# Loads between the halves of the stores, another order up to the second unit, and a last unit that ends in column parities over six banks

## The chip, the core and the metric

The kernel runs on one core of a Trainium2 chip. The core has five engines that each work through an instruction list of their own and meet at semaphores: PE (TensorE, matmul), DVE (VectorE), ACT (ScalarE), POOL (GpSimd) and SP (SyncE, which here only issues DMAs). The metric is the device time of one launch in microseconds (us). A profiled execution comes with a trace, from which all rows below are read.

## The reference

Two layers. Layer 0 takes x of shape (4, 256, 64, 64), convolves it 7x7 with dilation 2 to 128 channels, maps these to 49 logits for each pixel, takes a softmax over the 49, and sums the 49 shifted copies of x with these weights:

```python
k = conv(x, w1, padding=6, rhs_dilation=2) + b1
k = conv(k, w2) + b2                       # 1x1, 49 outputs
attn = softmax(k, axis=1)
y0 = einsum('bkchw,bkhw->bchw', shifts(x, 49), attn)
```

Layer 1 adds to y0 a gelu of `yc + y0 * D`, where `yc` comes from a linear recurrence over the 64 columns, and takes a layernorm over the 256 channels with a scale and a shift:

```python
y = gelu(yc.T[None, :, None, :] + x * D[None, :, None, None])
o = layernorm_over_channels(x + y) * ln_w + ln_b
```

## The kernel before

Both weights of layer 0 are folded into one 7x7 convolution with 48 outputs (softmax needs only differences of logits). Since the dilation is 2, even and odd rows are independent: the work falls into eight **units** (4 images x 2 row parities), unit n being image n // 2, parity n % 2. x of a unit lies in `raw0` or `raw1` by parity. The convolution runs over transformed rows (a scheme that trades multiplications for sums of rows): DVE and POOL build eleven arrays from `raw` (`make_u1` and its like, lines 1028 to 1041 and 313), ACT writes the f16 high part of each (`v_high`, line 700) and DVE the low part (`v_low`, line 1110), in a ring of four buffers `V`. PE convolves them in `conv(n, first, last)`, 49 steps in seven blocks of seven (line 438). Block b waits for the arrays that it reads and, in the first unit, for the weights' low parts (`weights_low`, line 1436; `weights_high` is ACT's, line 866).

What follows the convolution of unit m = n - 1 is done beside the convolution of unit n:

1. logits from the sums (`logits_*`, lines 1149 and 1158), turned by PE (`turn_logits`, line 457), gathered by DVE (1208, 1210), exponentials on ACT, sixteen small ones (737), division and a high and a low half (742, 1230), turned again (467) and copied to `AT` (746);
2. `spread(m, r)`, ten rows r: PE spreads the weights to a banded matrix in one of two PSUM banks `wk` (478), ACT casts it (`band_high`, 751), DVE makes the rest (`band_low`, 1235);
3. `apply(m, y)`, eight of them (495): PE multiplies the band with the turned x (`XT`) into one of two banks; y runs over row half q, channel half h, column parity w. ACT evicts each (`attended`, 760), DVE makes the arguments of gelu (1250), ACT the gelu (766), DVE the residual (1256);
4. the layernorm: POOL sums the channel halves (338, 344), PE the channels with a matrix of ones (`mean` 509, `variance` 516), DVE centres and normalises (1263, 1269), ACT squares, inverts and applies scale and shift (773, 781, 787). The second half of unit m ends in unit n + 1.

SP issues all loads of x and all stores, in one written order. In `unit(n)` it waits until unit n - 1's x is no longer read (`pool_rows`, `xt_done`), loads x of unit n + 1, and then waits four times for the output of unit n - 1 (`affine`) and stores it, two DMAs for each row half. So the load of x(n + 2) stands behind the second half of these stores. Readers of a new x are, in this order on their engines: ACT's `bound` (line 725, the largest absolute value, between `band_high` 4 and 5, and 6 and 7), from which POOL's all-reduce (309) and DVE's `scales` (1116) follow, and DVE's `make_u1` (1028, between `band_low` 2 and 3).

The **first unit** has the weights' preparation in front and in between: composites on PE (603), row sums on DVE (1367, `row_sums`), x turned by PE (`turn_x`, 529) with ACT's and DVE's halves behind (731, 1139). PE turns x in eight places from step 16 of the convolution on. The order of all engines there is written out by hand, as it is in `unit`.

The **last unit** has no convolution beside its steps 1 to 4. Its layernorm works in quarters (`last_centre`, `last_squares`, `last_rstd`, `last_normalise`, `last_affine`).

## Time and profile before

| | |
|---|---|
| median of 3 runs | 895.67 us (894.84 to 896.17) |
| profiled execution | 896.21 us, its span 894.4 us |
| PE busy | 803.0 us (90%) |
| DVE busy | 722.4 us (81%) |
| ACT busy | 519.9 us (58%) |
| POOL busy | 188.4 us (21%) |
| share of PE in the chain that ended last | 51% |
| DMA of x in that chain | 7% |
| mean granted clock of TensorE | 0.947 of full speed |

The span is what the trace covers from the first to the last instruction; 1.8 us of the profiled execution lie around it. A share of busy time is an average over three stretches that differ: the first unit (until about 146 us), six units with a period of some 97 us, of which five are followed by another load, and the end of the last one (from about 820 us), where PE has no convolution. What a change is worth is read in each of them. In a timeline a number in brackets is the time that the engine waited before the row, and behind the arrow stands what ended it ("issue": nothing that the trace shows).

### The profile page before, as it was taken

The page shows a single profiled execution, that of the slowest core. Times are in us where ns is not written, and L with a number is a line of the kernel's source. Part 1 is how long each engine was busy: PE and PEld are TensorE (multiplying, and loading weights), DVE is VectorE, ACT ScalarE, POOL GpSimd, SP SyncE. Part 2 cuts the span into 40 slices and gives each one's busy share as a digit, 9 for nine tenths or more (in the row PEclk, how much of TensorE's full clock was granted, in tenths as well). Part 3 has the DMA queues.
Part 4 walks back from the last instruction along what each step waited for, and adds up shares of the span by engine and source line. Part 5 has one row for each costly group of instructions (what it writes and reads, how often), then busy time and mean ns, then how long its engine had stood idle before and what let it go on. Part 6 is the DMA issues. An engine that isn't in the chain of part 4 may idle for free.

```text
span 894.4 us, 27128 instructions
## 1 busy us (share of the span) xinstructions
PE 803.0 (90%) x12261; PEld 493.8 (55%) x12261; DVE 722.4 (81%) x876; ACT 519.9 (58%) x834; POOL 188.4 (21%) x100
## 2 busy tenths in 40 slices
PE   4979787999997999899997999899989999996485
PEld 4975333575555655565564645565546655663451
DVE  3899769889995999689986999599967999677336
ACT  2363232766674666665584767557665659465546
POOL 3114102112510233013311151024301341021010
PEclk9999889999997999999997999999997999999588
DMA  9322005000125010700151011601070011002103
GB/s 312 72 52 45 2 2 95 2 3 2 48 53 92 3 48 2 143 3 1 49 113 33 2 48 42 104 1 40 11 143 2 1 49 50 3 1 64 32 1 94
DMA packets 133597, 41.78 MB, mean 47 GB/s; under 512 B 133145, under 2 KB 133226, under 8 KB 133226
## 3 DMA queue, kind: packets, MB, share of 16 engines
q1 hardware_dynamic: 132248, 40.01, 19.9%
q8 instruction: 96, 1.57, 0.7%
q10 hardware_dynamic: 1234, 0.04, 0.1%
q14 instruction: 19, 0.16, 0.1%
HBM read 23.27 MB, written 16.78 MB: 45 GB/s over the span
## 4 chain that ended last, share of the span: by engine, by line
PE 51%; DVE 15%; issue 12%; ACT 11%; DMA 8%; POOL 1%; SPq 1%; DVEq 0%; ACTq 0%; POOLq 0%
PE cv L438 26%; DMA raw<-in_x_dram 7%; PE wk L495 6%; PE pcomp L603 5%; PE wk L478 4%; PE ms L516 3%; ACT chs L737 3%; ACT V L700 3%; PE wk L529 2%; DVE R L1028 2%; DVE tg L1250 2%; PE wk L457 2%; DVE V L1110 1%; DVE XT L1139 1%; DVE Z L1158 1%
## 5 line engine op out<-in xcount | busy, mean ns | idle before, releaser
L438 PE MATMUL cv<-V,W 128*32 128x496 f16 (+6 forms) x7840 | 447.1, 383 | 19.7 <-issue 7.5
L438 PEld LDWEIGHTS cv<-V,W 128*32 128x32 f16 (+1 forms) x7840 | 201.5, 97 | 224.7 <-issue 41.6
L313 POOL TENSOR_TENSOR R<-raw 128x1152 f32<-128x1152 f32 x32 | 100.2, 3130 | 258.4 <-DVE V L1110 93.8
L700 ACT ACTIVATE V<-R,sc 128x1024 f16<-128x1024 f32 (+1 forms) x88 | 110.5, 1274 | 55.1 <-PE cv L438 54.3
L1110 DVE SCALAR_TENSOR_TENSOR V<-R,sc,V 128x1024 f16<-128x1024 f32 (+1 forms) x88 | 122.4, 1399 | 9.7 <-ACT V L700 9.6
L478 PE MATMUL wk<-AT,sel 128*128 128x16 f16 x2560 | 85.1, 192 | 23.1 <-DVE band L1235 21.2
L495 PE MATMUL wk<-band,XT 128*128 128x224 f16 (+1 forms) x960 | 102.9, 268 | 2.6 <-DVE band L1235 1.4
L478 PEld LDWEIGHTS wk<-AT,sel 128*128 128x128 f16 x2560 | 79.6, 103 | 44.7 <-DVE band L1235 29.6
L495 PEld LDWEIGHTS wk<-band,XT 128*128 128x128 f16 x960 | 83.3, 99 | 25.5 <-issue 5.3
L1235 DVE TENSOR_TENSOR band<-wk,band 128x512 f16<-128x512 f32 x80 | 54.7, 689 | 44.0 <-ACT band L751 43.8
L751 ACT CAST band<-wk 128x512 f16<-128x512 f32 x80 | 46.7, 584 | 69.4 <-PE wk L478 68.4
L731 ACT ACTIVATE XT<-wk,sc 128x512 f16<-128x512 f32 x64 | 42.9, 681 | 53.6 <-PE wk L529 52.9
L760 ACT ACTIVATE o<-wk,sc 128x512 f32<-128x512 f32 x64 | 45.7, 730 | 46.7 <-PE wk L495 46.6
L1041 DVE SCALAR_TENSOR_TENSOR R<-R 128x1024 f32<-128x1024 f32 (+1 forms) x56 | 72.5, 1298 | 0.2
L1028 DVE SCALAR_TENSOR_TENSOR R<-raw 128x512 f32<-128x512 f32 (+1 forms) x48 | 48.2, 1047 | 27.5 <-DMA raw<-in_x_dram 27.4
L1139 DVE SCALAR_TENSOR_TENSOR XT<-wk,sc,XT 128x512 f16<-128x512 f32 x64 | 47.2, 746 | 16.5 <-ACT XT L731 16.3
L338 POOL TENSOR_TENSOR chs<-o 128x1024 f32<-128x1024 f32 x14 | 36.7, 2622 | 110.4 <-DVE o L1256 95.1
L344 POOL TENSOR_TENSOR chs<-tg 128x1024 f32<-128x1024 f32 x14 | 34.5, 2462 | 96.3 <-ACT tg L773 96.3
L603 PE MATMUL pcomp<-w2t,w1raw 128*128 128x48 f32 x196 | 45.0, 418 | 9.4 <-DMA w1raw<-in_L_conv_w_dram 9.4
L1250 DVE SCALAR_TENSOR_TENSOR tg<-o,dcol,yc 128x1024 f32<-128x1024 f32 x32 | 40.4, 1279 | 13.4 <-ACT o L760 13.1
L529 PEld LDWEIGHTS wk<-id,raw 128*128 128x128 f32 x256 | 35.1, 208 | 27.9 <-issue 14.2
L603 PEld LDWEIGHTS pcomp<-w2t,w1raw 128*128 128x128 f32 x196 | 43.7, 312 | 10.0 <-issue 9.6
(138 smaller groups left out, 903.1 us busy)
## 6 DMA issues: line engine op xcount, KB each, us to landing
raw<-in_x_dram SPq DMA_DIRECT2D x16, 1024.0 KB, 11.5
out_dram<-o SPq DMA_DIRECT2D x28, 512.0 KB, 3.9
w1raw<-in_L_conv_w_dram SPq DMA_DIRECT2D x2, 3136.0 KB, 16.8
out_dram<-o SPq DMA_DIRECT2D x8, 256.0 KB, 3.4
cm<-in_L_conv_Cmat_dram ACTq DMA_DIRECT2D x1, 32.0 KB, 8.4
dcol<-in_L_conv_D_dram ACTq DMA_DIRECT2D x2, 0.5 KB, 9.8
lnw<-in_L_conv_ln_w_dram ACTq DMA_DIRECT2D x2, 0.5 KB, 7.2
lnb<-in_L_conv_ln_b_dram ACTq DMA_DIRECT2D x2, 0.5 KB, 7.2
```

Source lines behind the costliest of these rows:

```text
L313: nc.gpsimd.tensor_tensor(R[buffer][:, :, :, :], rows_of(par, j + 2), rows_of(par, j), ALU.subtract).then_inc(pool_rows, 1)
L438: ins = pe.matmul(to.rearrange("p (w t c) -> p w t c", w=2, c=COLS)[:, :, :, c0:c1], W[:, ws, h * K7 + v, k0:k1], slot(n, a)[:, low, :, t0 ...
L478: ins = pe.matmul(wk[:, r % 2, c * TILES:(c + 1) * TILES].rearrange("p (w j) -> p w j", w=2), sel[:, s, f:f + P], AT[:, :, r:r + 29:4, c], ...
L495: ins = pe.matmul(wk[:, y % 2, (r0 - 16 * q) * COLS:(r1 - 16 * q) * COLS], XT[:, xl, 8 * w + j, h, :], band[:, bl, 8 * w + j, r0 - 4 * j + ...
L603: last = pe.matmul(pcomp[:, g % 3, v * P:v * P + REL], w1h[:, u * K7 + v, :], w2t[:, 0:REL], start=True, stop=True)
L700: nc.scalar.activation(v_array(n, a, 0), array(a), ACT.Identity, scale=sc[:, par, 3:4]).then_inc(vhi, 1)
L1028: nc.vector.scalar_tensor_tensor(out=R[buffer][:, 0:wins, h, :], in0=raw[par][:, h, r:r + 4 * wins - 3:4, :], scalar=-4.0, in1=raw[par][:, ...
L1041: nc.vector.scalar_tensor_tensor(out=part(*out), in0=part(*a), scalar=factor, in1=part(*b), op0=ALU.mult, op1=ALU.add).then_inc(row_made, 1)
L1110: nc.vector.scalar_tensor_tensor(out=v_flat(n, a, 1), in0=array_flat(a), scalar=sc[:, par, 3:4], in1=v_flat(n, a, 0), op0=ALU.mult, op1=AL ...
L1139: nc.vector.scalar_tensor_tensor(out=low, in0=wk[:, g % 2, :], scalar=sc[:, par, 3:4], in1=high, op0=ALU.mult, op1=ALU.subtract).then_inc( ...
L1235: nc.vector.tensor_tensor(band[:, 1, :, r, :], wk[:, r % 2, :].rearrange("p (c t) -> p t c", t=TILES), band[:, 0, :, r, :], ALU.subtract). ...
L1250: nc.vector.scalar_tensor_tensor(out=tg[:, h], in0=o[:, q, h], scalar=dcol[:, h:h + 1], in1=yc[:, h].unsqueeze(1).broadcast_to([P, 16, WID ...
```

## The change

Three parts, in one diff.

**A. SP.** `store` now stores one row half. Behind the first half of unit n - 1's output SP waits for `xt_done` and `pool_rows` and loads x of unit n + 2; the second half of the stores comes behind it.

**B. The first unit.** PE turns x before the convolution and earlier inside it, DVE and ACT do their parts of the same work in another order: `relative_bias` later, the turned x's low halves earlier, the rows of unit 1 before the last weights, `scales(1, 1)` before `v_low(0, 0, 10)`. ACT's bound of x(1) still waits for all weights. No arithmetic is added.

**C. The end of the last unit.** The two halves of the softmax go through separately, the second half's logits turned into `cv`, which the convolution no longer needs; PE runs 22 and 9 idle matmuls between (`keep_running`, their result is overwritten); `spread` and `apply` use six banks in place of two; ACT's eviction `attended` is gone, and DVE makes the arguments of gelu and the residual straight from PSUM for each of the eight column parities (`last_args`, `last_residual`, 128x512 each in place of four of 128x1024); gelu goes in eight parts.

The diff, cut to its core:

```diff
-            def unit(n, par, b_load, b_out):
+            def next_load(n, par, b):
                 sp.wait_ge(pool_rows, POOL_ROWS * n)
                 sp.wait_ge(xt_done, 8 * n)
-                load(n + 1, 1 - par, b_load)
-                store(n, par, b_out)
+                load(n + 1, 1 - par, b)
...
             load(1, 1, 0)
-            for n in range(1, UNITS - 1):
-                unit(n, n % 2, (n + 1) // 2, (n - 1) // 2)
-            store(7, 1, 3)
+            next_load(1, 1, 1)
+            for n in range(1, UNITS):
+                store(n, n % 2, (n - 1) // 2, 0)
+                if n < UNITS - 2:
+                    next_load(n + 1, (n + 1) % 2, (n + 2) // 2)
+                store(n, n % 2, (n - 1) // 2, 1)
...
-                if r >= 2:
-                    pe.wait_ge(blo, 10 * m + r - 1)
+                banks = 6 if m == LAST else 2
+                if r >= banks:
+                    pe.wait_ge(blo, 10 * m + r - banks + 1)
...
-            conv(0, 0, 16, cold=True)
-            for g in range(8):
-                turn_x(0, 0, g, cold=True)
-                conv(0, 16 + 4 * g, 20 + 4 * g, cold=True)
+            turn_x(0, 0, 0, cold=True)
+            turn_x(0, 0, 1, cold=True)
+            conv(0, 0, 6, cold=True)
+            turn_x(0, 0, 2, cold=True)
...
+            def keep_running(w):
+                if w == 0:
+                    pe.wait_ge(l_soft, 2)
+                for _ in range(IDLE_MATMULS[w]):
+                    pe.matmul(wk[:, 0, 0:5 * 2 * REL], id16[:, :], W[:, 0, 0:5, :].rearrange("p s k -> p (s k)"),
+                              start=True, stop=True)
...
+            def last_high(w):
+                act.wait_ge(l_soft, (13, 17)[w])
+                nc.scalar.copy(HL[:, w * WIN:(w + 1) * WIN, 0:TAPS], E[:, w * WIN:(w + 1) * WIN, :]).then_inc(l_hi, 1)
...
+            def last_args(y):
+                h, w = y // 2 % 2, y % 2
...
+                dve.wait_ge(y_done, 8 * m + y + 1)
+                nc.vector.scalar_tensor_tensor(out=tg[:, h, :, w:WIDTH:2],
+                                               in0=apply_bank(m, y).rearrange("p (r c) -> p r c", c=COLS),
+                                               scalar=ds[:, h:h + 1],
+                                               in1=yc[:, h, w:WIDTH:2].unsqueeze(1).broadcast_to([P, 16, COLS]),
+                                               op0=ALU.mult, op1=ALU.add).then_inc(l_args, 1)
```

What stands on the engines at three places. First SP, from the load of x(2) on; `raw` is x, `out_dram<-o` a store. Before:

```order
L274 DMA raw<-in_x_dram 128x32x64 [waits x_turned,pool_rows]
L274 DMA raw<-in_x_dram 128x32x64
L280 DMA out_dram<-o 128x16x64 [waits affine_done] x4
L274 DMA raw<-in_x_dram 128x32x64 [waits x_turned,pool_rows]
L274 DMA raw<-in_x_dram 128x32x64
L280 DMA out_dram<-o 128x16x64 [waits affine_done] x4
```

And now, on SP at the same place:

```order
L287 DMA raw<-in_x_dram 128x32x64 [waits x_turned,pool_rows]
L287 DMA raw<-in_x_dram 128x32x64
L293 DMA out_dram<-o 128x16x64 [waits affine_done] x2
L287 DMA raw<-in_x_dram 128x32x64 [waits x_turned,pool_rows]
L287 DMA raw<-in_x_dram 128x32x64
L293 DMA out_dram<-o 128x16x64 [waits affine_done] x4
```

The load of x(3) has moved from behind four stores to behind two; the same holds for x(4) to x(7).

Second, DVE late in the first unit, where the scales of x(1) are made (1116 before, 1209 now, which waits for POOL's all-reduce `amax_all`). Before (1139 is the turned x's low half, 1028 rows of x(1)):

```order
L1110 SCALAR_TENSOR_TENSOR V<-R,sc,V 128x2x512 [waits rows_made,v_high]
L1028 SCALAR_TENSOR_TENSOR R<-raw 128x9x64 [waits v_low,raw_in_odd,borders_set]
L1028 SCALAR_TENSOR_TENSOR R<-raw 128x9x64
L1028 SCALAR_TENSOR_TENSOR R<-raw 128x8x64 [waits rows_made]
L1028 SCALAR_TENSOR_TENSOR R<-raw 128x8x64
L1036 TENSOR_TENSOR R<-R 128x1024 [waits rows_made,v_low]
L1036 TENSOR_TENSOR R<-R 128x1024 [waits rows_made]
L1158 SCALAR_TENSOR_TENSOR Z<-ev,Z 128x16x32 [waits logit_steps]
L1158 SCALAR_TENSOR_TENSOR Z<-Z 128x16x32 [waits logit_steps]
L1158 SCALAR_TENSOR_TENSOR Z<-ev,Z 128x16x32 [waits logit_steps]
L1158 SCALAR_TENSOR_TENSOR Z<-Z 128x16x32 [waits logit_steps]
L1116 TENSOR_SCALAR sc<-aall 128x1 [waits amax_all]
```

And now, on DVE from the last low half of the weights (1531) on:

```order
L1531 SCALAR_TENSOR_TENSOR W<-wc,wsc,W 128x7x16
L1203 SCALAR_TENSOR_TENSOR V<-R,sc,V 128x1152 [waits rows_made,v_high]
L1244 SCALAR_TENSOR_TENSOR ev<-cv,sc,ev 32x512 [waits logit_steps,block_convolved,sums_copied]
L1244 SCALAR_TENSOR_TENSOR Z<-cv,sc,ev 128x16x32 [waits logit_steps,block_convolved]
L1244 SCALAR_TENSOR_TENSOR ev<-cv,sc,ev 128x512 [waits logit_steps,block_convolved]
L1253 SCALAR_TENSOR_TENSOR Z<-ev,Z 128x16x32 [waits logit_steps]
L1253 SCALAR_TENSOR_TENSOR Z<-Z 128x16x32 [waits logit_steps]
L1124 TENSOR_TENSOR R<-R 128x1024 [waits rows_made,v_low]
L1209 TENSOR_SCALAR sc<-aall 128x1 [waits amax_all]
```

The rows of x(1) have moved ahead of the last weights, and the instruction that waits for `amax_all` stands eight rows behind these weights, where before the rows of x(1) and four combinations of logits (1158) came in between; `v_low(0, 0, 10)`, which stood ahead of it, now follows it.

Third, PE at the end of the last unit, from the turned logits to the first `spread`. Before:

```order
L457 MATMUL wk<-id,Z 128x128 [waits x_turned_low,logit_steps]
L457 MATMUL wk<-id,Z 128x128 x7
L457 MATMUL wk<-id,Z 128x128 [waits softmax_steps]
L457 MATMUL wk<-id,Z 128x128 x7
L467 MATMUL ms<-id,HL 128x128 [waits normed,softmax_steps]
L467 MATMUL ms<-id,HL 128x128 x7
L467 MATMUL ms<-id,HL 128x128 [waits normed,softmax_steps]
L467 MATMUL ms<-id,HL 128x128 x7
```

And now, on PE (699 are the idle matmuls, 705 the turned weights of one half each):

```order
L690 MATMUL wk<-id,Z 128x128 [waits x_turned_low,logit_steps]
L690 MATMUL wk<-id,Z 128x128 x7
L690 MATMUL cv<-id,Z 128x128 x8
L699 MATMUL wk<-W,id 128x480 [waits last_softmax_steps]
L699 MATMUL wk<-W,id 128x480 x21
L705 MATMUL cv<-id,HL 128x128 [waits last_softmax_steps]
L705 MATMUL cv<-id,HL 128x128 x7
L699 MATMUL wk<-W,id 128x480 x9
L705 MATMUL cv<-id,HL 128x128 [waits last_softmax_steps]
L705 MATMUL cv<-id,HL 128x128 x7
```

The second half's logits no longer wait for the first half's gather, and thirty-one idle matmuls have come in.

## Rows read from the trace of the kernel before

**Rows 1.** Windows: us; busy (xcount) of PE, PEld, DVE, ACT, POOL; PEclk, DMA share, GB/s
```profile
835.60:852.30 16.70, 12.38 (x336) 11.59 (x336) 6.91 (x10) 7.79 (x12) 0.00 (x0) 0.50 0.01 3
```

**Rows 2.** Waits of DVE, 245 to 735 us: us in total, times, longest us
```profile
DVE R L1028 <- DMA raw<-in_x_dram: 27.4, 5, 5.9
```

**Rows 3.** Waits of PE, 245 to 735 us
```profile
PE wk L478 <- DVE band L1235: 19.4, 5, 5.1
PE cv L438 <- issue: 2.3, 2, 1.5
```

**Rows 4.** Timeline of SP: start us, us, engine line op out<-in xcount [idle before <-releaser]
```profile
231.37 33.21 SPq L280 DMA_DIRECT2D out_dram<-o  x4
264.68 6.08 SPq L274 DMA_DIRECT2D raw<-in_x_dram  x2
```

**Rows 5.** Timeline of PE, unit 1
```profile
157.14 14.78 PE L438 MATMUL cv<-V,W 128*32 128x480 f16 x280
...
234.91 0.74 PE L529 MATMUL wk<-id,raw 128*128 128x128 f32 x4
```

**Rows 6.** Timeline of PE, unit 2
```profile
249.08 14.78 PE L438 MATMUL cv<-V,W 128*32 128x480 f16 x280
```

**Rows 7.** Timeline of PE, unit 7
```profile
735.70 14.78 PE L438 MATMUL cv<-V,W 128*32 128x480 f16 x280
...
773.85 6.24 PE L495 MATMUL wk<-band,XT 128*128 128x224 f16 x60
```

**Rows 8.** Timeline of DVE, unit 2
```profile
256.30 2.35 DVE L1269 TENSOR_TENSOR o<-o,ms 128x1024 f32<-128x1024 f32 x2
...
279.25 1.43 DVE L1028 SCALAR_TENSOR_TENSOR R<-raw 128x576 f32<-128x576 f32 x2 [5.49 <-DMA raw<-in_x_dram]
```

**Rows 9.** Waits of DVE, 47 to 149 us
```profile
DVE XT L1139 <- ACT XT L731: 9.2, 4, 4.2
DVE V L1110 <- ACT V L700: 6.3, 4, 3.2
```

**Rows 10.** Timeline of POOL, unit 1
```profile
189.38 0.37 POOL L309 PARTITION_ALL_REDUCE aall<-amx  x1 [22.44 <-ACT tg L725]
197.00 2.87 POOL L313 TENSOR_TENSOR R<-raw 128x1152 f32<-128x1152 f32 x1 [7.24 <-issue]
```

**Rows 11.** Timeline of ACT, first unit
```profile
117.65 1.90 ACT L725 ACTIVATE tg<-raw 128x2048 f32<-128x2048 f32 x1
...
119.54 1.30 ACT L700 ACTIVATE V<-R,sc 128x1152 f16<-128x1152 f32 x1
```

**Rows 12.** Timeline of DVE, first unit
```profile
120.88 1.42 DVE L1110 SCALAR_TENSOR_TENSOR V<-R,sc,V 128x1152 f16<-128x1152 f32 x1 [2.34 <-ACT V L700]
...
123.39 0.75 DVE L1149 SCALAR_TENSOR_TENSOR Z<-cv,sc,ev 128x512 f32<-128x512 f32 x1
...
132.15 2.49 DVE L1036 TENSOR_TENSOR R<-R 128x1024 f32<-128x1024 f32 x2
134.55 0.69 DVE L1158 SCALAR_TENSOR_TENSOR Z<-ev,Z 128x512 f32<-128x512 f32 x1
```

**Rows 13.** Timeline of PE, start of unit 1 behind the first unit
```profile
148.01 4.88 PE L438 MATMUL cv<-V,W 128*32 128x512 f16 x60 [2.99 <-DVE Z L1149]
```

**Rows 14.** Timeline of PE, last unit
```profile
838.68 2.10 PE L478 MATMUL wk<-AT,sel 128*128 128x16 f16 x64 [1.17 <-ACT AT L746]
841.22 2.10 PE L478 MATMUL wk<-AT,sel 128*128 128x16 f16 x64 [0.44 <-DVE band L1235]
...
852.36 8.89 PE L495 MATMUL wk<-band,XT 128*128 128x224 f16 x60 [1.40 <-DVE band L1235]
```

**Rows 15.** Timeline of ACT, last unit
```profile
826.95 0.34 ACT L737 ACTIVATE chs<-chs,st 128x49 f32<-128x49 f32 x1 [1.20 <-DVE st L1218]
...
875.59 1.28 ACT L1010 ACT_TABLE_LOAD   x1
876.89 0.66 ACT L987 ACTIVATE cv<-cv,eps 128x512 f32<-128x512 f32 x1
```

More of the change, by code:

```diff
@@ L190, in conv_seq_kernel @@
         ms16 = ms[:].bitcast(F16)
+        cv16 = cv[:].bitcast(F16)
+        last_banks = [wk[:, 0, :], wk[:, 1, :]] + [cv[:, i, :] for i in range(4)]
+        spread_bank = lambda m, r: last_banks[r % 6] if m == LAST else wk[:, r % 2, :]
+        apply_bank = lambda m, y: last_banks[(0, 1, 4, 5, 2, 3, 0, 1)[y]] if m == LAST else wk[:, y % 2, :]
+        var_bank = lambda i: cv[:, (i + 2) % 4, :]
         s_w1 = [sem("w1_in_0"), sem("w1_in_1")]
@@ L486, in apply @@
                     pe.wait_ge(blo, 10 * m + 10)
-                if y >= 2:
+                if m == LAST and y >= 6:
+                    pe.wait_ge(l_res, y - 5)
+                if m < LAST and y >= 2:
                     pe.wait_ge(xs_made, 8 * m + y - 1)
@@ L706, in sum_copy @@
                     act.wait_ge(z_step, steps)
+                if not n:
+                    act.wait_ge(s_bias, 4)
+                    act.wait_ge(scale_steps, SCALES)
                 add = bias[:, :] if s == M1P else 0.0
@@ L779, in inverse_deviation @@
                 act.wait_ge(var_done, 2 * m + q + 1)
+                if m == 0 and q == 0:
+                    act.wait_ge(s_const, 2)
                 both = ms[:].rearrange("p a b -> p (a b)")
@@ L861, in weights_high @@
             def weights_high(first, last):
+                if first == 0:
+                    act.wait_ge(amax_part, 2)
+                    act.wait_ge(s_wscale, 12)
                 for s, h in HIGH_ORDER[first:last]:
@@ L968, in _, with last_exponentials, last_turned, last_gelu @@
             m = UNITS - 1
-            inverse_deviation(m - 1, 1)
+            def last_exponentials(w, first, last):
+                act.wait_ge(l_soft, 5 * w + 5)
+                for i in range(w * WIN + first, w * WIN + last):
+                    nc.scalar.activation(E[:, i, :], E[:, i, :], ACT.Exp, bias=st[:, 1, i:i + 1],
+                                         accum_out=st[:, 2, i:i + 1]).then_inc(l_exp, 1)
+            def last_high(w):
+                act.wait_ge(l_soft, (13, 17)[w])
+                nc.scalar.copy(HL[:, w * WIN:(w + 1) * WIN, 0:TAPS], E[:, w * WIN:(w + 1) * WIN, :]).then_inc(l_hi, 1)
+            def last_turned(w):
+                act.wait_ge(ht_ready, 2 * m + w + 1)
+                nc.scalar.copy(AT[:, w, PAD:PAD + ROWS, :].rearrange("p r c -> p (r c)"), cv16[:, 2 + w, :]).then_inc(
+                    at_copy, 1)
+            def last_gelu(y):
+                h, w = y // 2 % 2, y % 2
+                act.wait_ge(l_args, y + 1)
+                nc.scalar.activation(tg[:, h, :, w:WIDTH:2], tg[:, h, :, w:WIDTH:2], ACT.Gelu).then_inc(l_gelu, 1)
+            inverse_deviation(m - 1, 1)
+            last_exponentials(0, 0, 8)
+            last_exponentials(1, 0, 4)
+            last_high(0)
+            last_exponentials(1, 4, 8)
+            last_turned(0)
+            last_high(1)
+            last_turned(1)
+            band_high(m, 0)
+            band_high(m, 1)
             scale_shift(m - 1, 1, 0)
+            band_high(m, 2)
+            band_high(m, 3)
             scale_shift(m - 1, 1, 1)
-            exponentials(m, 0, 16)
-            attention_high(m)
-            turned_attention(m, 0)
-            turned_attention(m, 1)
-            for r in range(BROWS):
+            for r in range(4, BROWS):
                 band_high(m, r)
@@ L1050, in make_u1 @@
                 for h in range(HALVES):
+                    if not n:
+                        dve.wait_ge(first_in[h], 16)
                     u_half(0, par, h, 2, 0, 9)
@@ L1129, in logit_scales @@
             def logit_scales(n, par):
+                if not n:
+                    dve.wait_ge(s_mask, 2)
                 nc.vector.tensor_scalar(sc[:, par, 4:5], sc[:, par, 1:2], winv[:, :], 1 / X_SCALE, ALU.mult,
@@ L1469, in _ @@
             weight_scales()
-            for h in range(HALVES):
-                dve.wait_ge(first_in[h], 16)
-            dve.wait_ge(s_border, 2)
             make_u1(0, 0)
@@ L1502, in _ @@
+            turned_x_low(0, 0, 0)
+            relative_bias()
+            turned_x_low(0, 0, 1)
+            weights_low(4, 11)
+            turned_x_low(0, 0, 2)
             v_low(0, 0, 4)
+            weights_low(11, 12)
+            turned_x_low(0, 0, 3)
+            weights_low(12, 14)
+            make_y2_plus(0)
             v_low(0, 0, 5)
-            make_y2_plus(0)
+            turned_x_low(0, 0, 4)
+            v_low(0, 0, 6)
+            weights_low(14, 15)
             make_y2_minus(0)
-            weights_low(12, 16)
@@ L1526, in _ @@
             logits_2(0, 0)
+            logits_rows(0, True)
+            make_x1_plus(1)
+            scales(1, 1)
             v_low(0, 0, 10)
-            dve.wait_ge(s_border, 4)
-            make_u1(1, 1)
-            make_u0(1, 1)
-            make_x1_plus(1)
+            logit_scales(1, 1)
             make_x1_minus(1)
-            logits_rows(0, True)
+            make_u2(1, 1)
             logits_rows(0, False)
-            scales(1, 1)
-            logit_scales(1, 1)
-            turned_x_low(0, 0, 5)
@@ L1568, in last_centre @@
                 dve.wait_ge(q_mean, i + 1)
-                dve.wait_ge(o_made, 4 * m + (2 if i < 2 else 4))
+                dve.wait_ge(l_res, 4 if i < 2 else 8)
                 for h in range(HALVES):
```

285 lines of the change are left out of this document (182 added, 103 removed).

## The prediction

> **What bounds the kernel now.** I read the shares on the page first (PE busiest, DVE next), then the windows by stage, since the three parts of the change lie in stages with different limits, then the waits in each stage, and at last the timelines at the places that the change moves.
>
> In the units PE is the bound but for one gap. From 245 to 735 us the waits of DVE have one entry that is large: five waits, one in each of units 2 to 6, for a load of x, 27.4 us in all [rows 2]. The waits of PE have its echo: 19.4 us in five waits for DVE's `band_low` [rows 3]. The reader is to see why in SP's timeline: the load follows the fourth store in the same row of the queue, at 264.68, though the first stores stood there at 231.37 [rows 4]. PE had turned the last of the old x at 234.91 + 0.74 = 235.65 [rows 5], and from then on the buffer was free. DVE stood at `make_u1` from 273.76 and went on at 279.25 [rows 8].
>
> In the first unit nobody is the bound alone. DVE waits 9.2 us for ACT's turned x and 6.3 us for ACT's `v_high` [rows 9], which wait for PE in turn; unit 1 starts on PE at 148.01, behind DVE [rows 13]. At the end PE, ACT and DVE hand each other small pieces; the windows show PE's clock at half there, 0.50 of full (1.2 GHz), from 835.6 to 852.3, though PE is busy 12.38 of 16.70 us [rows 1].
>
> **A, the load of x, units 2 to 6.** Two units show what a unit takes when x is there in time. The same place in the program, the 280 matmuls from step 5 on, begins at 157.14 in unit 1, at 249.08 in unit 2 and at 735.70 in unit 7 [rows 5 to 7]. Unit 1, whose x(2) had been loaded early, took 249.08 - 157.14 = 91.94 us. Units 2 to 6 took (735.70 - 249.08) / 5 = 97.32 each. The difference, 5.38 us, is more than PE's wait of 19.4 / 5 = 3.9, because the clock falls after the wait. Five units: 26.9 us.
>
> Is unit 1 a fair pattern? It lacks the second half of the layernorm of the unit before; on DVE that is two instructions, 2.35 us [rows 8], on ACT and PE about as much. They stand well ahead of `make_u1`, where the next wait is one for exponentials, so I take nothing off for them; if they came onto the path, 2.35 x 5 = 11.8 would be gone. Unit 1 also has no load in flight. In units 2 to 6 PE has two pauses with no releaser, 2.3 us together [rows 3]. In future PE has no slack to hide such pauses, and I keep them whole: 26.9 - 2.3 = 24.6. On SP the two issues of the load, 6.08 us [rows 4], stand ahead of the second stores, which were not through before 264.68; with its issues from 235.65 to 241.7 the load is out of their way. The load itself comes 264.68 - 235.65 = 29.0 us earlier, against the 5.49 that were missing, so there are some 23 us to spare. Bounds of A: 12.8 (the layernorm's share and the pauses both lost) and 27.4, DVE's whole wait.
>
> On the pauses the Trainium skill, page "SBUF — State Buffer", section "SBUF: two separate sides", holds that DMA ports and engine ports cannot slow each other. By that rule A would be the full 26.9; the two pauses are of the sequencer and not of data, so the rule may be right and the pauses stay all the same.
>
> **B, the first unit.** The work is conserved; DVE has no pause but 9.2 + 6.3 = 15.5 us of waits [rows 9]. Since unit 1 begins when DVE is through, B is worth the waits that vanish, less those that come. All turned-x waits are of PE's late `turn_x`; in the new order PE turns early and DVE's pieces are due when their inputs are old. But one new wait stands out. ACT's bound of x(1) still needs the last low half of the weights, and DVE's `scales(1, 1)` now stands soon behind it. From the last low half: bound 1.9 + 0.2, `v_high` 1.30, bound again [rows 11] (the second as the first), together 5.3; then the all-reduce. Its own row is 0.37 long, but POOL's next instruction, which waits for nothing new, comes 7.6 us after its start [rows 10]. That makes 12.9. On DVE meanwhile: `v_low` 1.42, three sums at 0.75, two combinations at 0.69 and one `make_x1_plus` at 1.24 [rows 12], 6.3 in all. DVE would stand 6.6 us, and behind it queue `v_low(0, 0, 10)`, on which PE's last block waits, and everything for unit 1. One more us for small new waits, which I can't place: 15.5 - 6.6 - 1.0 = 7.9. Bounds: if the all-reduce's result is out after its own 0.37 us, it comes 5.3 + 0.4 = 5.7 behind the weights, before DVE is there at 6.3, and B is 14.5; if PE and ACT's new places (ACT now waits for a turned x ahead of weights) cost as much as they bring, B is 0, and a little below it, -3, if one such wait of 3 us is left. I take the middle one, since POOL's gap is the nearest row.
>
> **C, the last unit.** Three steps, on the way to the table load at 875.59, behind which the quarters go on as before: the inversion starts at 876.89 [rows 15], and from it to the end of the execution I change nothing.
> 1. From the turned logits to the first `spread`. Before, the first exponential is at 826.95 [rows 15] and the first spread at 838.68 [rows 14], 11.7 apart: sixteen exponentials at 0.33 are 5.2, the rest 6.5. Now the first half's exponentials need only the first gather (they start some 4.0 earlier, as the second half's turning, its gather and two layernorm instructions of 2.35 in all [rows 8] are no longer ahead), and behind the sixteenth only the second half's pieces remain, each half as long, about 4.1. That is 4.0 + 2.4 = 6.4.
> 2. Ten spreads. Two take 2.10 and then wait 0.44 for a bank [rows 14], so ten with what follows took 852.36 - 838.68 = 13.7. With six banks 10 x 1.05 + 1.3 for the last cast and low half = 11.8. Gain 1.9. ACT has two late scale-and-shifts among its casts; a cast is shorter than a spread, and it catches up.
> 3. From the first `apply` to the table load: before 875.59 - 852.36 = 23.2. Now eight applies at 6.24 / 4 = 1.56, the rate of unit 7 [rows 7], are 12.5, one mean of ones 1.1 among them, then an argument 0.75, a residual 0.75, a centring 1.3 and the squares 1.3 (512 columns at 0.65 to 0.75, as rows 12 and 15): 17.7. Gain 5.5. DVE has 16 pieces of 0.75 = 12.0, just under PE's 12.5.
>
> That is 13.8. It holds only at full clock. Four applies took 8.89 right behind the spreads, against 6.24 [rows 7, 14]: 2.65 for the half clock. The spreads did not raise the clock before [rows 1], there are ten of them in a row again, and the idle matmuls end before them. I take it that the clock is down again when `apply` begins: C = 13.8 - 2.65 = 11.2. Bounds: 14 above; below 5, if DVE, which now has evictions too, paces step 3 and nothing is gained in it. The idle matmuls cost nothing if they are over when the halves come; an apply has 15 matmuls of 237 columns in the mean (96 to 320) in 1.56 us, so one of 480 takes 0.21 and 22 take 4.6, in a gap of some 6 (first gather to first half's weights).
>
> **Sum.** The profiled execution is 896.21. 896.21 - 24.6 - 7.9 - 11.2 = 852.5. The median of the runs shown lies 0.5 below that execution, so 852.
>
> **Rivals.**
> - *Everything mild goes well*, 0.2: the clock stays at full through the spreads (+2.65), the all-reduce is soon out (+6.6), the pauses vanish (+2.3): 840.5. For it: before, PE had next to nothing to do between the turned logits and the turned weights, and the idle matmuls now fill that. Against: rows 1 show a busy PE that stays at half. The Trainium skill, page "TensorE: Matmul & The Clock Gate", section "What's actually happening", says that throttled is the default and that activity releases it; by it PE would keep the full clock from the idle matmuls on, and C alone would be 13.8.
> - *The layernorm's second half takes the place of the load*, 0.12: A is 24.6 - 11.8 = 12.8, 864. Against: unit 7 has that half too and its first `apply` comes 773.85 - 735.70 = 38.15 after the mark [rows 7], without wait for it.
> - *The first unit's order brings nothing*, 0.1: 860. For it: ACT now has in-order waits for turned x in front of weights that DVE needs.
> - *The last unit is paced by DVE*, 0.1: C is 5, 858.
> - *The load does not come earlier after all*, 0.02: SP reaches it only when `xt_done` is there, which might be late; A is 0, 877. Rows 5 and 8 speak against.
> - *Slower*, 0.03: the load now runs beside the end of one unit and the start of the next. If a load in flight kept PE from its instructions, PE would stand for its length. From issue to DVE's going on a load took 279.25 - 264.68 = 14.6 [rows 4, 8]; five are 73, against 43.7 gained: 925. It decides from 43.7 / 5 = 8.7 us a load on. Against: the pauses come to 0.5 a load now.
>
> **How the numbers follow.** My forecast, 852, has 0.43, with 846 to 858 as its own range. A difference under 0.2%, 1.8 us, can't be told from no change here; no case but a mixture reaches it. Faster 0.96, same 0.01, slower 0.03. The range holds forecast, the good case and the three bad ones in part: 838 to 865.
>
> **What would show it.** SP's load at the end of PE's eighth turned x and no wait of DVE's `make_u1` for a DMA; marks 92 to 93 us apart in units 2 to 6 (97.3 would refute A, 94.5 be the layernorm). Unit 1 starting about 140 on PE, and on DVE a wait of some 6 us ahead of `scales(1, 1)`. In the last unit the first spread some 6 us sooner behind the turned logits, the table load some 17 behind the first apply, and the clock in the window of the first applies: 0.5, or else 1.0. A PE busy share that does not rise to about 93% or more would mean that the time went elsewhere.

## The result, and the profile after

The changed kernel takes 834.11 us (833.27 to 835.22, four runs) against 895.92 for the kernel before on the same chip: 0.9305 of it, with a 95% interval of 0.9277 to 0.9332. The forecast was 852, and 834.11 lies below its range. The profiled execution took 833.81 us, 62.4 less than that of before, with a span of 832.0. In its profile PE is busy for 95% of the span and DVE for 87%.

The timeline of PE gives the marks again (start us, us, engine line op out<-in xcount [idle before <-releaser]). The mark of a unit is the start of its 280 matmuls from step 5 on, the same place in each unit's program. Shown are those of units 1, 2 and 7, and behind them the last unit's first spread, the first apply matmuls and their followers.

```profile
135.62 14.78 PE L454 MATMUL cv<-V,W 128*32 128x480 f16 x280
226.73 14.78 PE L454 MATMUL cv<-V,W 128*32 128x480 f16 x280
...
686.50 14.78 PE L454 MATMUL cv<-V,W 128*32 128x480 f16 x280
...
783.64 2.11 PE L495 MATMUL wk<-AT,sel 128*128 128x16 f16 x64 [1.10 <-ACT AT L1051]
...
794.86 4.81 PE L514 MATMUL wk<-band,XT 128*128 128x224 f16 x30 [1.41 <-DVE band L1330]
799.51 6.23 PE L514 MATMUL cv<-band,XT 128*128 128x224 f16 x60
```

Beside [rows 5 to 7] they divide the 62.4 us over the parts:

- up to the mark of unit 1: 157.14 - 135.62 = 21.5 (B, forecast 7.9)
- unit 1 itself: 91.94 before, 91.11 now: 0.8 (forecast 0). With one part alone it takes 91.97 to 91.99 (e1, e2 and e3 below), so no part gives this by itself, and its cause stays open
- units 2 to 6: (686.50 - 226.73) / 5 = 91.95 each against 97.32, so 26.8 (A, forecast 24.6)
- from the mark of unit 7 to the end of the span: 894.4 - 735.70 = 158.7 before, 832.0 - 686.50 = 145.5 now: 13.2 (C, forecast 11.2)

So the miss of 18.7 us (62.4 for a forecast of 43.7) is 13.6 from B, 2.2 from A, 2.0 from C and 0.8 from unit 1.

**A.** The timeline of SP answers to [rows 4].

```profile
209.02 3.47 SPq L293 DMA_DIRECT2D out_dram<-o  x2
213.38 5.37 SPq L287 DMA_DIRECT2D raw<-in_x_dram  x2
238.80 3.43 SPq L293 DMA_DIRECT2D out_dram<-o  x2
```

The load stands between the halves of a store, and it is issued as PE's eighth turned x ends (at 212.55 + 0.75 = 213.30), as the prediction asked. The waits of DVE in units 2 to 6 (226 to 687 us) hold no DMA any more ([rows 2] had 27.4 us), and the waits of PE have neither `band` nor a pause without a releaser ([rows 3] had 19.4 and 2.3). The largest entry of DVE now, and both entries of PE:

```profile
DVE band L1330 <- ACT band L814: 21.7, 29, 1.7
```
```profile
PE wk L548 <- DVE XT L1234: 4.3, 5, 0.9
PE ms L528 <- POOL chs L354: 1.2, 5, 0.2
```

The reader is to see that a large wait (21.7 us of DVE, for ACT's casts) stands beside a PE that waits for next to nothing.

**B.** The windows show DVE's way from the scales of unit 0 into unit 1, before and after (us; busy of PE, PEld, DVE, ACT, POOL; PEclk, DMA share, GB/s).

```profile
47.80:147.80 100.00, 79.89 (x1081) 46.12 (x1080) 83.19 (x135) 38.84 (x51) 17.55 (x10) 0.95 0.21 38
```
```profile
47.70:126.40 78.70, 74.48 (x1089) 46.06 (x1092) 75.06 (x134) 40.54 (x56) 17.15 (x10) 1.00 0.32 55
```

Both windows end some 0.65 us ahead of the same `v_low` (148.43 before, 127.07 now). The second is 21.3 us shorter, and in two ways: DVE's idle time went from 16.8 to 3.6 us (13.2), and its busy time, for the same work but one instruction of 0.75, from 83.19 to 75.06 (8.1). Of the 3.6 us of idle time that are left 2.4 are waits for ACT's `v_high`, 0.3 is the one for the all-reduce, and the rest lies between rows; the waits for turned x are gone.

**C.** These are the steps of the prediction. The first spread came 838.68 - 735.70 = 102.98 behind the mark of unit 7 and comes 97.14 behind it (5.8, forecast 6.4). Ten spreads with what follows took 13.7 and take 11.2 (2.5, forecast 1.9). From the first apply to the table load it was 23.2 and is 813.26 - 794.86 = 18.4 (4.8, forecast 5.5 less 2.65 for the clock). In the timeline of ACT:

```profile
813.26 1.28 ACT L1098 ACT_TABLE_LOAD   x1
814.55 0.66 ACT L1084 ACTIVATE cv<-cv,eps 128x512 f32<-128x512 f32 x1
```

From there to the end 17.5 us pass, as before. The windows of the last unit show the granted clock: full while the idle matmuls run, half again through the spreads and into the first applies.

```profile
772.00:783.60 11.60, 8.16 (x52) 4.00 (x50) 8.96 (x21) 8.97 (x37) 0.00 (x0) 1.00 0.01 2
783.60:794.90 11.30, 9.85 (x321) 9.75 (x322) 6.64 (x10) 8.53 (x13) 0.00 (x0) 0.54 0.39 96
794.90:799.50 4.60, 4.60 (x30) 3.41 (x31) 0.75 (x1) 1.05 (x2) 0.00 (x0) 0.64 0.00 0
799.50:805.60 6.10, 6.10 (x65) 5.19 (x63) 5.50 (x8) 2.64 (x5) 0.00 (x0) 1.00 0.02 4
```

### The profile page after: what moved, and what is told of

It reads as the page before. It is cut to its first block, busy times and chain, and to the rows that moved or that the text cites. A ratio compares the mean times of both kernels' runs of the same rounds, so it can differ in the third digit from the quotient of the medians.

```text
span 832.0 us, 27209 instructions
## 1 busy us (share of the span) xinstructions
PE 790.7 (95%) x12292; PEld 492.6 (59%) x12292; DVE 721.3 (87%) x892; ACT 514.8 (62%) x831; POOL 189.4 (23%) x100
## 4 chain that ended last, share of the span: by engine, by line
PE 59%; DVE 24%; issue 7%; ACT 7%; DMA 1%; POOL 1%; DVEq 0%; SPq 0%; ACTq 0%
PE cv L454 32%; PE wk L495 7%; PE pcomp L622 5%; DVE tg L1345 3%; PE ms L535 3%; DVE Z L1253 3%; PE wk L514 3%; PE wk L548 3%; DVE R L1116 3%; DVE V L1203 2%; DVE XT L1234 2%; DVE R L1124 2%; DVE Z L1244 2%; PE wk L473 1%; ACT tg L788 1%
## 5 line engine op out<-in xcount | busy, mean ns | idle before, releaser
L454 PE MATMUL cv<-V,W 128*32 128x496 f16 (+6 forms) x7840 | 429.9, 374 | 3.1 <-DVE V L1203 2.2
L514 PE MATMUL wk<-band,XT 128*128 128x224 f16 (+1 forms) x900 | 95.9, 267 | 1.4 <-DVE band L1330 1.4
L514 PEld LDWEIGHTS wk<-band,XT 128*128 128x128 f16 x900 | 77.6, 99 | 23.0 <-issue 5.1
L495 PEld LDWEIGHTS wk<-AT,sel 128*128 128x128 f16 x2368 | 73.6, 100 | 18.7 <-issue 16.6
L1330 DVE TENSOR_TENSOR band<-wk,band 128x512 f16<-128x512 f32 x74 | 51.0, 690 | 35.3 <-ACT band L814 34.9
L495 PE MATMUL wk<-AT,sel 128*128 128x16 f16 x2368 | 78.7, 192 | 1.1 <-ACT AT L1051 1.1
L814 ACT CAST band<-wk 128x512 f16<-128x512 f32 x74 | 43.1, 582 | 46.0 <-PE wk L495 45.0
L823 ACT ACTIVATE o<-wk,sc 128x512 f32<-128x512 f32 x56 | 40.1, 731 | 33.7 <-PE wk L514 33.6
L1116 DVE SCALAR_TENSOR_TENSOR R<-raw 128x512 f32<-128x512 f32 (+1 forms) x48 | 52.7, 1140 | 0.0
L548 PE MATMUL wk<-id,raw 128*128 128x128 f32 x256 | 43.3, 303 | 6.8 <-DVE XT L1234 5.1
L622 PEld LDWEIGHTS pcomp<-w2t,w1raw 128*128 128x128 f32 x196 | 43.7, 312 | 9.8 <-issue 9.4
```

The source lines that it names most:

```text
L454: ins = pe.matmul(to.rearrange("p (w t c) -> p w t c", w=2, c=COLS)[:, :, :, c0:c1], W[:, ws, h * K7 + v, k0:k1], slot(n, a)[:, low, :, t0 ...
L495: ins = pe.matmul(spread_bank(m, r)[:, c * TILES:(c + 1) * TILES].rearrange("p (w j) -> p w j", w=2), sel[:, s, f:f + P], AT[:, :, r:r + 2 ...
L514: ins = pe.matmul(apply_bank(m, y)[:, (r0 - 16 * q) * COLS:(r1 - 16 * q) * COLS], XT[:, xl, 8 * w + j, h, :], band[:, bl, 8 * w + j, r0 - ...
L548: ins = pe.transpose(wk[:, g % 2, c:c + P], rows[:, w:4 * WIDTH:2], id32[:, :])
L622: last = pe.matmul(pcomp[:, g % 3, v * P:v * P + REL], w1h[:, u * K7 + v, :], w2t[:, 0:REL], start=True, stop=True)
L1116: nc.vector.scalar_tensor_tensor(out=R[buffer][:, 0:wins, h, :], in0=raw[par][:, h, r:r + 4 * wins - 3:4, :], scalar=-4.0, in1=raw[par][:, ...
```

## The experiments

The theory: the 13.6 us that B brought beyond its forecast have two sources. The result of the all-reduce is out as soon as its row ends, and DVE's rows are no longer held while GpSimd (POOL) works. The rivals: the 13.6 come from another part of the change, or the rows are shorter for another reason.

### One part at a time

e1, the kernel before with SP's part (A) alone:

```
-            def store(n, par, b):
-                for q in range(2):
...
+            next_load(1, 1, 1)
+            for n in range(1, UNITS):
+                store(n, n % 2, (n - 1) // 2, 0)
+                if n < UNITS - 2:
+                    next_load(n + 1, (n + 1) % 2, (n + 2) // 2)
+                store(n, n % 2, (n - 1) // 2, 1)
```

> The kernel before with part A alone (SP's queue: each load of x between the two halves of a store). After's marks give part A 26.9 us (unit pitch 97.32 before, 91.95 after). If the parts add up, this one is at 895.7 - 26.9 = 869, with a pitch of 91.9 to 92.0 in units 2 to 6, a first unit and a last unit as before. If part A needs the other two (the layernorm's second half comes onto the path without them), the pitch is 94 or more and the time 880 or more.

868.19 us (866.28 to 868.71), 0.9701 of before (0.9671 to 0.9730), before at 895.22. That is 27.0 us, with the mark of unit 2 at 248.82 and of unit 7 at 707.72: a pitch of 91.8. A needs nothing of the rest, and the layernorm's second half doesn't come onto the path.

e2, the kernel before with the new order of ACT, DVE and PE up to the second unit alone:

```
-            conv(0, 0, 16, cold=True)
-            for g in range(8):
-                turn_x(0, 0, g, cold=True)
...
+            turn_x(0, 0, 0, cold=True)
+            turn_x(0, 0, 1, cold=True)
+            conv(0, 0, 6, cold=True)
...
```

> The kernel before with part B alone (the order of ACT, DVE and PE up to the second unit). My theory now: part B is worth 21 to 22 us (13 of waits, 8 of DVE instructions that no longer run beside one of POOL's), so 874. As the prediction priced it: 7.9, so 888. The rival, that the rest of the 21.5 seen in after comes from somewhere else (the changed queue of SP, or the spread of one execution): 880 or more. The mark of unit 1 on PE is at 135.6 by the first, 149 by the second.

874.67 us (872.86 to 875.54), 0.9774 (0.9745 to 0.9804): 20.6 us, mark of unit 1 at 134.88, 22.3 before that of [rows 5]. So what B brought beyond its forecast is B's own.

e3, the kernel before with the end of the last unit alone:

```
-            turn_logits(m, 0)
-            turn_logits(m, 1)
...
+            last_logits(0)
+            last_logits(1)
+            keep_running(0)
...
```

> The kernel before with part C alone (the end of the last unit). From the mark of unit 7 to the end of the span: before 158.7, after 145.5. If the parts add up: 895.7 - 13.2 = 882.5. If part C owes something to the earlier parts (a queue of stores that is less behind), less: 885 to 890.

885.68 us (881.41 to 888.13), 0.9895 (0.9851 to 0.9939). Its profile has 881.5 - 734.78 = 146.7 from the mark of unit 7 to the end, 12.0 less than before. The time says 9.5, with four runs spread over 6.7 us, which doesn't decide between the two expectations. By the times the three parts alone sum to 57.1 us, the whole to 61.8. With e3's interval of 3.9 us to either side that is no proof that the parts help each other. By the marks of the profiled executions they sum to 27.7 + 22.3 + 12.0 = 62.0 against 62.4, so the parts add up there.

### The all-reduce

e5, the changed kernel with the all-reduce for x(1) done twice:

```
+                if n == 1:
+                    nc.gpsimd.partition_all_reduce(aall[:, par, :], amx[:, par, :], P, ABSMAX).then_inc(again, 1)
+                    pool.wait_ge(again, 1)
                 nc.gpsimd.partition_all_reduce(aall[:, par, :], amx[:, par, :], P, ABSMAX).then_inc(amax_all, 1)
```

> The changed kernel with the all-reduce for x(1) done twice, the second waiting for the first. My theory now: a result is out 1.3 us after the start (in after DVE goes on 1.26 after it), so DVE's stall ahead of scales(1, 1) grows from 0.26 to about 1.6 and unit 1 starts some 1.3 us later: 835.5. By the prediction's price (7.6 us from start to the next thing on POOL) the second result comes 7 to 8 us later: 841.

835.23 us (833.30 to 836.55), 0.9318 (0.9293 to 0.9344). The timelines of POOL and of DVE in the changed kernel, and then in e5:

```profile
113.23 1.23 POOL L325 PARTITION_ALL_REDUCE aall<-amx  x1 [14.18 <-ACT tg L788]
```
```profile
105.42 2.52 DVE L1531 SCALAR_TENSOR_TENSOR W<-wc,wsc,W 128x224 f16<-128x224 f32 x8
...
113.01 1.22 DVE L1124 TENSOR_TENSOR R<-R 128x1024 f32<-128x1024 f32 x1
114.49 0.21 DVE L1209 TENSOR_SCALAR sc<-aall 128x1 f32<-128x1 f32 x1 [0.26 <-POOL aall L325]
```
```profile
112.87 1.26 POOL L327 PARTITION_ALL_REDUCE aall<-amx  x1 [14.14 <-ACT tg L792]
114.23 0.36 POOL L329 PARTITION_ALL_REDUCE aall<-amx  x1
```
```profile
114.63 0.21 DVE L1213 TENSOR_SCALAR sc<-aall 128x1 f32<-128x1 f32 x1 [0.73 <-POOL aall L329]
```

In both the result is out when POOL's row ends: 1.26 us after its start in the one, 0.40 in the second of e5. The stall grows by 0.5 instead of 1.3, since the second row is the shorter one, and the mark of unit 1 is at 135.75, 0.13 later. (The time, 835.23, came near the expected 835.5, but its interval overlaps that of the changed kernel, and the stall doesn't account for the 1.1.) The price of 7.6 us is refuted, and so is my new one as a constant: it is the row's own length. That was 0.37 for all seven in the kernel before. The long ones, 1.23 and 1.26, both started 0.2 us behind a combination of DVE from SBUF to SBUF (113.01 above, 112.68 in e5) and ended 0.2 behind it. That fits the next section, the all-reduce being held by DVE there; no run moves the one away from the other.

### DVE beside GpSimd

The timelines of the kernel before, POOL and then DVE, hold what the prediction passed over: the same kind of row in two lengths.

```profile
62.14 2.77 POOL L313 TENSOR_TENSOR R<-raw 128x1152 f32<-128x1152 f32 x1 [29.82 <-DVE R L1036]
69.15 2.77 POOL L313 TENSOR_TENSOR R<-raw 128x1152 f32<-128x1152 f32 x1 [4.24 <-DVE V L1110]
...
81.55 3.58 POOL L313 TENSOR_TENSOR R<-raw 128x1152 f32<-128x1152 f32 x1 [6.96 <-DVE V L1110]
107.86 3.69 POOL L313 TENSOR_TENSOR R<-raw 128x1152 f32<-128x1152 f32 x1 [22.74 <-issue]
```
```profile
61.98 3.67 DVE L1436 SCALAR_TENSOR_TENSOR W<-ut,wsc,W 128x224 f16<-128x224 f32 x4
...
68.99 3.67 DVE L1436 SCALAR_TENSOR_TENSOR W<-ut,wsc,W 128x224 f16<-128x224 f32 x4
...
73.78 2.35 DVE L1041 SCALAR_TENSOR_TENSOR R<-R 128x1024 f32<-128x1024 f32 x2
...
81.39 4.82 DVE L1041 SCALAR_TENSOR_TENSOR R<-R 128x1024 f32<-128x1024 f32 x2
...
109.64 5.45 DVE L1436 SCALAR_TENSOR_TENSOR W<-wc,wsc,W 128x224 f16<-128x224 f32 x12
```

Four low halves of weights took 3.67 us beside a subtraction of GpSimd (POOL's line 313), and 1.30 without one (54.43). Two combinations took 4.82 beside one and 2.35 alone. Three such places cost 2.4 each, and a fourth (twelve low halves at 109.64, 5.45 us instead of some 3.8) 1.6 more: 8.9 in all. In the changed kernel two of the four subtractions cost DVE nothing: they fall beside row sums out of PSUM (58.23) and beside turned x and logits out of PSUM (96.40). The other two, POOL and then DVE:

```profile
67.11 3.65 POOL L329 TENSOR_TENSOR R<-raw 128x1152 f32<-128x1152 f32 x1 [6.25 <-DVE V L1203]
...
83.25 2.65 POOL L329 TENSOR_TENSOR R<-raw 128x1152 f32<-128x1152 f32 x1 [9.82 <-DVE V L1203]
```
```profile
70.04 4.88 DVE L1531 SCALAR_TENSOR_TENSOR W<-ut,wsc,W 128x224 f16<-128x224 f32 x14
...
84.73 2.25 DVE L1203 SCALAR_TENSOR_TENSOR V<-R,sc,V 128x1024 f16<-128x1024 f32 x1 [0.90 <-ACT V L757]
```

One `v_low` took 2.25 instead of 1.28. Of the fourteen low halves the first took 0.98, for 0.32 or 0.44 of the others, while the end of the subtraction ran (to 70.76): 0.5. That is 1.5 in all. GpSimd's memsets, which only write, are no part of it: in the kernel before they ran from 71.86 to 74.59 beside a `v_low` that took 1.27 and the start of the two combinations that took 2.35. The difference of 7.4 and the one instruction of 0.75 are the 8.1.

e6 and e7 put one and two more subtractions beside DVE work from SBUF to SBUF, e8 a smaller one beside row sums out of PSUM:

```
+            def extra(rows, times):
+                for i in range(times):
...
+                    nc.gpsimd.tensor_tensor(spare[:, 0:rows * WIDTH],
+                                            raw0[:, 0, 2:2 + rows, :].rearrange("p r w -> p (r w)"),
+                                            raw0[:, 0, 4:4 + rows, :].rearrange("p r w -> p (r w)"),
+                                            ALU.subtract).then_inc(late_cleared, 1)
...
+            pool.wait_ge(vlo, 5)
+            extra(18, 1)          # e7: extra(18, 2); e8: extra(12, 1) ahead of make_c2(0, 0)
             make_w(0, 0)
```

> The changed kernel with one more subtraction of 128x1152 on GpSimd, of rows of x into a buffer that nobody reads, about 78.3 us, while DVE computes low halves of weights from SBUF to SBUF. Theory (DVE stands while GpSimd works, if both of DVE's tensors are in SBUF): the DVE rows beside it take 2.4 us more in all, of which 0.9 goes into the wait for ACT at 84.73, so unit 1 starts 1.5 to 2.4 later: 836. Rival (the 8 us that DVE's rows lost have another reason, e.g. fewer cold starts or DMA beside them): no DVE row longer than 0.1 beyond its kind, 834.1.

> The same with two such subtractions, one behind the other. Theory: DVE's rows 4.8 us longer, unit 1 3.5 to 4.8 later, 838. Rival: 834.1.

> The changed kernel with one more subtraction on GpSimd, of 128x768, about 61 us, where DVE sums rows out of PSUM (L1462, eight in a row, 58.9 to 62.7). Theory: DVE isn't held where one of its tensors is in PSUM; those rows stay at 0.50 each, at most 0.5 us is lost on the low half of weights behind them, 834 to 834.5. If GpSimd holds DVE whatever it reads: 1.8 us more, 836.

e6: 836.47 us (835.31 to 837.66), 0.9337 (0.9308 to 0.9365). e7: 838.65 (837.36 to 840.17), 0.9359 (0.9335 to 0.9383). e8: 834.57 (833.58 to 835.21), 0.9312 (0.9289 to 0.9334). The same place in the timeline of DVE, two low halves, in the changed kernel and in e6, with e6's POOL between them:

```profile
78.27 0.70 DVE L1531 SCALAR_TENSOR_TENSOR W<-ut,wsc,W 128x224 f16<-128x224 f32 x2
```
```profile
78.33 2.85 POOL L407 TENSOR_TENSOR band<-raw 128x1152 f32<-128x1152 f32 x1 [4.47 <-DVE V L1216]
```
```profile
78.16 3.16 DVE L1544 SCALAR_TENSOR_TENSOR W<-ut,wsc,W 128x224 f16<-128x224 f32 x2
```

The two low halves take 2.5 us more, and the last 280 matmuls of unit 0 on PE start at 112.53 instead of 110.20 (2.3 later), in e7 at 115.24 (5.0 later, a little more than expected). The rows carry this; of the times alone, e6's interval still overlaps that of the changed kernel, and e7's does not. In e8, POOL and then DVE:

```profile
60.65 1.85 POOL L407 TENSOR_TENSOR band<-raw 128x768 f32<-128x768 f32 x1
```
```profile
58.72 3.89 DVE L1475 SCALAR_TENSOR_TENSOR ut<-pcomp,ut 128x336 f32<-128x336 f32 x8
```

The eight row sums take 3.89 with it and 3.86 without. So in these runs DVE stands for as long as GpSimd's subtraction lasts where both of its tensors are in SBUF, and not where one is in PSUM. The Trainium skill, page "SBUF — State Buffer", section "Who interferes with whom", states this: a DVE instruction with both inputs in SBUF contends with a GpSimd one that reads SBUF, the one that comes second blocks until the first is through, and with at most one such input (outside DVE's two-port modes) there is no contention. The runs agree, with 2.5 us and 0.03 us; on which of the two goes first, one row of e12 differs (last section).

e12, the kernel before with its first such subtraction held until DVE's low halves are through:

```
+            pool.wait_ge(w_low, 12)
             make_c0(0, 0)
             make_c2(0, 0)
```

> The kernel before with GpSimd's first late subtraction (62.14 there) held until DVE's low halves of weights at 61.98 are through, so that it runs beside a row sum out of PSUM. Theory: DVE's four low halves take 1.3 again instead of 3.67, so DVE is 2.4 us earlier at 66; and of this nothing or little is left at the start of unit 1 (157.1 for its mark), because DVE waits for the turned x at 93.31 and 102.15 anyway: the time stays at 895. Rival (the shorter rows pay by themselves): 892.9, mark of unit 1 at 154.7.

892.30 us (888.28 to 895.46, twelve runs), 0.9966 (0.9949 to 0.9983): some 3 us faster, as the rival said, and my theory, that the waits behind would absorb the gain, fell. The timeline of DVE in e12, then that of the kernel before at the same wait:

```profile
61.77 1.30 DVE L1437 SCALAR_TENSOR_TENSOR W<-ut,wsc,W 128x224 f16<-128x224 f32 x4
...
98.56 0.75 DVE L1140 SCALAR_TENSOR_TENSOR XT<-wk,sc,XT 128x512 f16<-128x512 f32 x1 [4.11 <-ACT XT L732]
```
```profile
102.15 0.75 DVE L1139 SCALAR_TENSOR_TENSOR XT<-wk,sc,XT 128x512 f16<-128x512 f32 x1 [4.17 <-ACT XT L731]
```

The wait of 4.17 at 102.15 is 4.11 at 98.56. The longest waits don't absorb the gain, they move with it. I explain that by what they wait for: PE's turned x stands behind convolutions, and these wait for DVE's own low halves. PE's first convolution bears this out, in e12 and in the kernel before:

```profile
64.83 18.53 PE L439 MATMUL cv<-V,W 128*32 128x512 f16 x320 [2.94 <-issue]
```
```profile
67.41 19.49 PE L438 MATMUL cv<-V,W 128*32 128x512 f16 x320 [5.29 <-issue]
```

It starts 2.6 us earlier, in both 1.76 behind the end of those four low halves, and PE turns its first x 3.5 earlier (83.29 for 86.83). The 320 matmuls themselves took 1.0 less, which no run here explains. The mark of unit 1 is at 153.74 instead of 157.14. So one held place of 2.4 us was worth 3.4 at the start of unit 1.

### The clock and the banks of the last unit

e4, without the idle matmuls:

```
-IDLE_MATMULS = (22, 9)
+IDLE_MATMULS = (0, 0)
```

> The changed kernel without its 31 idle matmuls in the last unit. In after the clock is at full over 772 to 783.6 and at 0.54 over the spreads (783.6 to 794.9), and the first thirty matmuls of apply took 4.81 instead of 3.1. Theory: the clock falls in the spreads with or without idle matmuls, and the spreads take 1.05 at either clock, so the idle matmuls are worth only what the transposes of the attention gain, under 1 us: 834 to 835. Rival: without them the clock is down for more of the applies, as before (8.89 for four, 2.65 over), and the time is 836 to 838.

834.54 us (833.15 to 836.58), 0.9336 (0.9303 to 0.9370). Windows of e4:

```profile
771.00:783.60 12.60, 2.70 (x38) 2.20 (x39) 8.37 (x20) 8.39 (x37) 0.00 (x0) 0.60 0.00 1
783.60:794.90 11.30, 9.90 (x309) 9.63 (x306) 6.63 (x10) 9.00 (x13) 0.00 (x0) 0.50 0.38 97
```

From the start of the first turned logits to the first spread 13.08 us became 13.97; behind that all is alike (the first thirty apply matmuls 4.75 against 4.81). The 31 idle matmuls are worth 0.9 us in the trace, which the times don't tell from nothing.

e9, spreads over two banks again:

```
-                banks = 6 if m == LAST else 2
+                banks = 2
```

> The changed kernel with the last unit's spreads over two banks again, all else as changed. Theory: the banks are the whole of the spreads' gain (13.7 before, 11.2 after), so the first apply comes 2.5 us later: 836.6. Rival: with ACT and DVE rid of the late layernorm pieces, two banks are enough: under 1 us.

837.36 us (835.36 to 837.55), 0.9346 (0.9322 to 0.9369). From the first spread to the first apply it is 797.68 - 783.96 = 13.7, as before the change. The waits of 0.44 to 0.47 are back behind every second spread: the banks are the whole of that step.

e10, e11 and e13 put idle matmuls elsewhere:

```
+            def more_idle(times):
+                pe.wait_ge(normed, 4 * m + 4)
+                for _ in range(times):
+                    pe.matmul(ms[:, 0, 0:5 * 2 * REL], id16[:, :], ...)
...
             for r in range(BROWS):
                 spread(m, r)
+            more_idle(4)          # e10, e15; e13 also with IDLE_MATMULS = (0, 0); e11: one behind each spread
```

> The changed kernel with four more idle matmuls of 480 columns behind the last spread, into a bank of the layernorm's mean, in the 1.4 us in which PE waits for the last low half of the bands. Theory: at half clock they take 1.6 us, push the first apply by 0.2 to 0.4, and the clock rises no sooner by much: first thirty matmuls of apply 4.0 to 4.8, time 833.5 to 834.5. If the clock is up at once: 3.1, time 832.5.

> The changed kernel with one more idle matmul of 480 columns behind each of the spreads 1 to 9 (and two behind the last). The spreads take 1.05 at either clock, so all that a full clock can give is the 1.7 us of the first applies. Theory: the idle matmuls keep the clock up but cost 9 x 0.2 to 0.4 on PE, which paces the spreads: first applies at 3.1, spreads 2 to 3 us longer, time 834 to 836. Rival: they fit into the 0.1 to 0.2 between spreads and the time falls to 832.5.

> The changed kernel without its 31 idle matmuls, but with four behind the last spread. In e10 the four ran at half clock in the gap and the applies behind them came back 1.3 us sooner. Theory: the four alone do it: as e10, 832.8. Rival: the 31 have to come first, so 834.1 or more.

> The changed kernel itself, beside the others on the same chip: 834.1, first thirty matmuls of apply at 4.8 us.

> The version with the 31 and the four, once more: first thirty matmuls of apply at 3.5 us, 1.0 to 1.5 us below the changed kernel in the same set of runs.

| run | us | the first thirty apply matmuls, us |
|---|---|---|
| e10, four behind the spreads | 832.82 (831.35 to 835.17) | 3.52 |
| e15, the same again | 833.24 (830.98 to 835.03) | 4.92 |
| e14, the changed kernel again | 833.85 (833.67 to 834.44) | 5.72 |
| e13, the four alone | 834.75 (834.29 to 835.08) | 4.38 |
| e11, one behind each spread | 837.37 (836.46 to 838.30) | 4.75 |

Against before, e15 is at 0.9301 (0.9275 to 0.9326) and e14 at 0.9311 (0.9286 to 0.9336). That the version with the four is faster is not shown. The expectations that I drew from e10's one profile all fell: e13 was to be 832.8, e15 to have its first applies at 3.5 and to lie 1.0 to 1.5 us below e14 (it lies 0.6 below), and e14's own first applies took 5.72 for 4.8. They take between 3.5 and 5.7 us in these profiles, the changed kernel's own two differing by 0.9, and what decides that is open. In e11 the clock was at 0.57 from 783 to 800 us, though nearly every spread had a matmul of 480 columns behind it, and first spread to first apply was 799.40 - 785.04 = 14.4 instead of 11.2: against my theory they did not keep the clock up, and they bought nothing.

## Why the prediction was wrong

The forecast of 43.7 us of gain was 18.7 too small, and most of that lies in B, in two steps of its working.

- **A was right** in mechanism; the size was 2.2 short. The two pauses that I kept (2.3 us) went with the wait. The full 26.9 was what followed from the rule of the Trainium skill's page "SBUF — State Buffer", section "SBUF: two separate sides"; 26.8 was measured, 27.0 by the times with that part alone.
- **B failed in two terms.** The first: "DVE would stand 6.6 us", which is 0.26. All else in that chain held: the all-reduce starts 5.3 us behind the last low half of the weights (107.94 to 113.23), and DVE has its 6.3 us of other work (to 114.23). Only the result's price was wrong, 1.26 for 7.6. I took the start of POOL's *next* instruction in [rows 10] for the end of this one. The other value that I had, the row's own 0.37, was nearly the truth, and I gave it no place but the bound of 14.5 and a rival of 0.2. This term is 6.3 of the miss. Some 1.1 goes the other way: DVE's remaining idle time is 3.4, where I had 1.0, but before it was 16.8, where I had 15.5.
- The second: "The work is conserved; DVE has no pause but 9.2 + 6.3". The work is conserved, its duration is not. In the kernel before 8.9 us of DVE's busy time was DVE held beside GpSimd, and 7.4 of these went. I had put this term at nothing without looking at the rows. No bound held it, so 14.5 was no upper end (21.5 measured). It could have been seen in the stretch of [rows 9], by one kind of row in two lengths.
- **C was right** within 2: the banks brought 2.5 for 1.9, the first step 5.8 for 6.4. The clock was down at the first applies, as forecast; its cost was 4.81 - 6.23 / 2 = 1.7 and not 2.65. The other 1.0 of step 3 is spread over the applies and the pieces behind them, which took a little less than I had put. By the Trainium skill's page "TensorE: Matmul & The Clock Gate", section "What's actually happening", I let the clock stay up in a rival; the windows show 0.54 over the spreads and refute that use of it.
- **The rivals.** *Everything mild goes well* was the nearest: the pauses are gone and the all-reduce is soon out. Its clock did not stay up, and it still missed by 6 us, since it had no term for DVE held beside GpSimd. The others fell. *Layernorm*: the pitch is 91.95. *First unit brings nothing*: it brings 21.5. *DVE paces the end*: step 3 gained 4.8. *The load not earlier*: no wait for `raw` is left. *Slower*: PE has no pause beside the loads.

## What to carry over

The busy time of an engine is not its work. Before calling a reordering neutral, list the engine's rows by kind: where one kind has two lengths, look what another engine does beside the long ones. The result of an instruction is priced by its own row and by who takes it, not by when the next one on its engine starts. And a wait need not absorb what is saved ahead of it: look first whether what it waits for depends on the waiting engine's own earlier work, as in e12.
